# Eight relu evictions per supertile moved from ScalarE to VectorE in a fused attention and FFN kernel

## The reference, cut to what is computed

```python
xn = layernorm(x)
# attention branch: q, k, v = split(xn @ Wqkv); attention over the lags 0, 1, 2, 4, ...;
# a 7-tap causal convolution over v; linear attention with elu(q)+1, elu(k)+1; then @ Wo
x_prev = shift_by_one_token(xn)
xr = mu_r * xn + (1 - mu_r) * x_prev
xk = mu_k * xn + (1 - mu_k) * x_prev
r = sigmoid(xr @ W_r.T)
k = xk @ W_k.T
k_act = square(relu(k))
ffn = r * (k_act @ W_v.T)
y = x + (xn + attention) + ffn
```

## Time and profile before

| what | us |
|---|---|
| median of 2 runs (2105.49 to 2115.18) | 2110.34 |
| the profiled execution's own time | 2121.86 |
| its span on core 1, the slowest, which the rows are from | 2120.3 |
| spans of the eight cores | 2078.9 to 2120.3 |
| mean granted TensorE clock of core 1 | 0.839 |

### The profile page before, as it was taken

One profiled execution on the slowest core, in us unless ns is written; L12 is line 12 of the kernel. 1 busy time (PEld: TensorE's weight loads), 2 busy tenths in 40 slices (PEclk: granted clock), 3 DMA queues, 4 the chain that ended last, 5 costly groups with the idle time before them and its releaser, 6 DMA issues.

```text
span 2120.3 us, 32484 instructions; the slowest of 8 cores (2078.9 to 2120.3 us)
## 1 busy us (share of the span) xinstructions
PE 1433.3 (68%) x10400; PEld 815.1 (38%) x10400; DVE 1232.1 (58%) x1968; ACT 745.1 (35%) x992; POOL 118.4 (6%) x137
## 2 busy tenths in 40 slices
PE   0068778687887787868878715575757575758485
PEld 0024334334333343333343303343545463728282
DVE  0086487684884866848747466372727262636354
ACT  0034142242242422422324215253635362625263
POOL 0001001001010010010100100000000000000000
PEclk9999799788898797888879757788878887979797
DMA  8821320320403204113021262414141414132221
GB/s 150 112 70 50 79 105 16 111 89 15 154 31 90 100 11 129 71 36 133 31 77 73 60 164 56 129 31 130 31 130 30 130 32 129 32 113 48 80 71 40
DMA packets 75229, 168.08 MB, mean 79 GB/s; under 512 B 38080, under 2 KB 38208, under 8 KB 69952
## 3 DMA queue, kind: packets, MB, share of 16 engines
q1 hardware_dynamic: 59632, 100.98, 16.7%
q0 software_dynamic: 15440, 65.02, 11.6%
HBM read 113.55 MB, written 67.11 MB: 85 GB/s over the span
## 4 chain that ended last, share of the span: by engine, by line
PE 43%; DVE 18%; DMA 17%; issue 11%; ACT 9%; DVEq 1%; SPq 1%; POOL 0%; ACTq 0%; POOLq 0%
DVE s_cv L282 6%; PE PS L541 6%; DMA s_vr<-vt_sp 6%; PE PS L598 5%; PE PS L569 5%; PE PS L906 3%; PE PS L1071 3%; PE PS L1074 3%; PE PS L467 3%; DMA s_q<-q_sp 3%; PE PS L955 3%; PE PS L628 2%; PE PS L958 2%; PE PS L910 2%; DMA s_wq<-wqkv 2%
## 5 line engine op out<-in xcount | busy, mean ns | idle before, releaser
L467 PE MATMUL PS<-s_xnfm,s_wq 128*128 128x512 bf16 x1536 | 383.9, 413 | 60.8 <-ACT s_vh L490 43.2
L282 DVE SCALAR_TENSOR_TENSOR s_cv<-s_vh,s_cw,s_cv 128x512 bf16<-128x512 bf16 x384 | 328.1, 854 | 43.7 <-DVE s_cv L282 4.1
L926 DVE RECIPROCAL s_rr<-PS 128x512 f32<-128x512 f32 x64 | 214.9, 3358 | 126.8 <-PE PS L910 126.6
L973 ACT ACTIVATE s_er<-PS,s_con 128x768 bf16<-128x768 f32 (+5 forms) x256 | 226.8, 889 | 163.4 <-PE PS L958 162.9
L467 PEld LDWEIGHTS PS<-s_xnfm,s_wq 128*128 128x128 bf16 x1536 | 157.9, 104 | 283.7 <-issue 131.7
L955 PE MATMUL PS<-s_q,s_kr 128*128 128x128 bf16 x1288 | 186.1, 230 | 96.5 <-DMA s_q<-q_sp 79.4
L958 PE MATMUL PS<-s_id,s_mlog 128*128 128x128 bf16 x1288 | 187.0, 231 | 0.0
L906 PE MATMUL PS<-s_er,s_vr 128*128 128x128 bf16 x1288 | 119.0, 225 | 98.2 <-ACT s_er L973 68.1
L955 PEld LDWEIGHTS PS<-s_q,s_kr 128*128 128x128 bf16 x1288 | 132.9, 104 | 102.9 <-issue 100.6
L393 PE MATMUL PS<-s_id,s_xnb 128*128 128x128 bf16 x256 | 29.9, 283 | 159.9 <-DVE s_st L379 134.2
L958 PEld LDWEIGHTS PS<-s_id,s_mlog 128*128 128x128 bf16 x1288 | 133.5, 104 | 0.1
(11 more groups left out here) (99 smaller groups left out, 1827.7 us busy)
## 6 DMA issues: line engine op xcount, KB each, us to landing
s_xa<-x SPq DMA_DIRECT2D x32, 512.0 KB, 4.3
s_xb<-x SPq DMA_DIRECT2D x32, 512.0 KB, 4.4
p_sp<-s_p POOLq DMA_DIRECT2D x32, 512.0 KB, 3.7
s_p<-p_sp SPq DMA_DIRECT2D x32, 512.0 KB, 13.8
y<-s_p SPq DMA_DIRECT2D x32, 512.0 KB, 3.9
q_sp<-s_qk POOLq DMA_DIRECT2D x8, 1024.0 KB, 4.3
k_sp<-s_qk POOLq DMA_DIRECT2D x8, 1024.0 KB, 4.3
vt_sp<-s_vt POOLq DMA_DIRECT2D x8, 1024.0 KB, 8.1
```

The source lines that it names most:

```text
L282: cinc(e.scalar_tensor_tensor(s1_cv[:, ch, :], src, s_cw[:, ch, j:j + 1], s1_cv[:, ch, :], ALU.mult, ALU.add))
L467: last = e.matmul(bank(bsel, 0, 512), s1_wq[:, kc, 128 * m:128 * (m + 1)], s1_xnfm[:, kc, 1:513], start=(kc == 0), stop=(kc == 7), skip_gr ...
L926: cinc(e.reciprocal(s2_rr[:, 512 * half:512 * half + 512], PS[:, 512 * (6 + half): 512 * (6 + half) + 512]))
L973: return e.activation(s2_er[:, eslot, 0:128 * n], src, AF.Exp, bias=s_con[:, 0:1], scale=s_con[:, 1:2])
```

## The change

The relu of the W_k product moves from ScalarE (activation) to VectorE (tensor_scalar with max 0), with the same operands. The square on POOL, the reuse of the PSUM banks and the first four groups of the W_v product now wait for VectorE's count.

```diff
-            wts.append(("act", ka_evac[m - 4]) if m >= 4 else ("act", rg_evac[4 + m]))
+            wts.append(("dve", mx_done[m - 4]) if m >= 4 else ("act", rg_evac[4 + m]))
             W("tensor", kmm_fn, waits=wts, inc="pe")
             kmm = pl.val["pe"]
-            W("scalar", (lambda m, bsel: lambda e: e.activation(
-                s1_xr[:, m, :], bank(bsel, 0, 512), AF.Relu))(m, bsel),
-                waits=[("pe", kmm)], inc="act")
-            ka_evac[m] = pl.val["act"]
+            W("vector", (lambda m, bsel: lambda e: e.tensor_scalar(
+                s1_xr[:, m, :], bank(bsel, 0, 512), 0.0, None, ALU.max))(m, bsel),
+                waits=[("pe", kmm)], inc="dve")
+            mx_done[m] = pl.val["dve"]
             W("gpsimd", (lambda m: lambda e: e.tensor_tensor(
                 s1_xr[:, m, :], s1_xr[:, m, :], s1_xr[:, m, :], ALU.mult))(m),
-                waits=[("act", ka_evac[m])], inc="pool")
+                waits=[("dve", mx_done[m])], inc="pool")
...
-                wts.append(("act", ka_evac[4 + m]))
+                wts.append(("dve", mx_done[4 + m]))
```

## The result

The changed kernel takes 2148.01 us in the median (11 runs, 2143.6 to 2166.11) where the kernel before took 2107.46 beside it (8 runs, 2101.21 to 2118.95). The ratio is 1.0202, with a 95% interval of 1.0167 to 1.0238: the kernel is slower, and whether by more or by less than 2% is not settled. The forecast was 2154 us. In some executions of these kernels the cores of one die run at a lower granted clock and the time is some per cent longer; all times and ratios here leave those out. The ratios are worked out from the single runs and not from the medians, and the two can differ by 0.2 or 0.3%.

The account below looks back on a forecast made before the run. TensorE was taken as the bound, with a hole of 2.2 us per supertile waiting for the square. Later start plus clock, (3.8 + 1.7) x 8 = 44 us, on the 2110.34 us median gave 2154 us; range 2130 to 2180.

Parts of the forecast that it names:

- What bounds the stage: Second supertile's chain from W_k through relu and square to W_v: TensorE is the bound, with one hole, 2.2 us per supertile.
- The hand-over from VectorE to TensorE: Between W_k and W_v: late relus and four squares in a row start TensorE 3.8 us later in each supertile.
- its cover: Head 3 ends about 361.7, and the bank is needed at 363.8 at the earliest: covered by about 1.4 us.
- Relus 4 to 7. These are what the change costs: Relus queued behind head 2 on VectorE: all four late, in a row from 351.36, delaying squares and W_v by 3.8 us.
- they cost nothing: Relus 0 to 3, behind head 1 on VectorE: run at TensorE's pace with 3 us of cover, at no cost.
- The clock: W_v product behind the longer hole: starting at 1.2 GHz costs 2.1 us per supertile, less 0.4 paid now, adding 1.7.
- Nothing downstream takes the shift back: Stages behind the W_v product, from transposes to stores, start from what ended ahead of them and recover none of the delay.
- the fourth rival: First sweep's later stages: a changed clock pattern gives the loss back, 2119 us with all of it returned; chance 0.05.
- The squares alone: Rival 1, hole ahead of W_v: the deeper hole costs no more clock, 30 us in all, 2141 us; chance 0.22.
- Relu and square in turns: Rival 2, relus 4 to 7 and POOL's squares: they take turns, 64 us in all, 2174 us; chance 0.13.
- Head 3 holding up the squares: Rival 3, last two squares: each waits for a head 3 operation, 1.8 us more, 2168 us; chance 0.09.
- The squares' steady 1.04 us does not show the turn in which POOL waits: POOL's squares beside two-input VectorE operations: minimum 1.03, median 1.04 us, so the rows show only VectorE stretching.

Follow-up runs that it names:

- The filled hole: Changed kernel with 24 matmuls whose results nobody reads in TensorE's hole between the W_k and W_v products: 2134.31 us, ratio 1.0142.
- the two with the product split: W_v's first two groups split, steps 0 to 6 ahead: kernel before, 2085.21 us; all relus on VectorE with head 2 ahead of them, 2099.15 us.

## Why the prediction was right, point by point

**What bounds the stage** was right: the chain through relu, square and W_v, with TensorE's hole of 2.1 us as its only gap. The wait was forecast to grow to about 48 us in 8 waits and is 46.0.

**The hand-over from VectorE to TensorE** was worked out as 3.8 us and measured as 3.58 (all cores). Its pieces: the relu 0.69 and 0.69; head 2 with one square beside it 6.62 and 6.30 (351.97 to 358.27); four squares 4.32 and 4.52; the hand-over 0.25 and 0.25. The stall of a head per square was taken as 0.76 from two heads beside eight squares; one square cost 0.44 here, and three cost 0.69 each in the experiment with relus 4 and 5 on ScalarE. Head 3, forecast at about 8 us, takes 7.20 (360.68 to 367.87), and its cover held.

**"Relus 4 to 7. These are what the change costs"** was wrong as an attribution, although the sum came out. Relus 4 to 7 alone on VectorE give a ratio of 0.9986. What fails is "they cost nothing" of relus 0 to 3: the cover of 3 us was read for the relus themselves and not for head 2, which the fourth of them holds from 335.7 to 344.7. The prediction has this delay in its next paragraph ("only then does head 2 start") and counts it, so the path and the sum are right; it books the whole cost on relus 4 to 7, because the wait appears only behind head 2.

**The clock** was taken as 2.1 us per supertile less 0.4 paid already. Over eight cores it is 16.20 - 13.97 = 2.23 less 0.29, so 1.94 against 1.7. The prediction read the 0.4 from core 1, which had two slow starts in eight. The filled hole shows that this term is the clock's and not a second wait.

**"Nothing downstream takes the shift back"** held as far as the traces can tell. The W_r product and the rest together are 0.55 us shorter per supertile, 4 us of 44, a tenth of what the fourth rival needed, and even these can't be put down to the change, since the rest is as short in two kernels whose W_v product runs near full clock. The rest does react to something, though. In the three kernels without a hole of 2 us ahead of the W_v product (the hole filled, and the two with the product split) the rest takes 91.84 to 92.00 us; in the other six it takes 91.17 to 91.55. The projections alone do not explain it: their matmuls have a mean of 409 ns with the hole filled and 404 with the product split. The cause stays open.

**The total** came out 3 us low: a loss of 41 us by the medians, against the forecast's 44. The other 3 us between 2154 and 2148 are the starting point, 2110.34 us in the two runs that the forecast had and 2107.46 beside the result.

**Rivals 1 to 3.** The squares alone: refuted, the W_v product takes 15.3 to 16.9 us in all 64 cases and not 14. Relu and square in turns: refuted by the line of the relu in the changed kernel (durations in ns: shortest, median, longest), with squares running beside many of them:

```profile
L577 DVE TENSOR_SCALAR s_xr<-PS x64: 679/691/693, 200.1 to 1212.0; 128x512 bf16<-128x512 f32 x64
```

Head 3 holding up the squares: this happens, at a fifth of the rival's 1.8 us. These are one operation of head 3 and the eighth square, in the second supertile of core 0:

```profile
361.39 1.34 DVE L282 SCALAR_TENSOR_TENSOR s_cv<-s_vh,s_cw,s_cv 128x512 bf16<-128x512 bf16 x1
362.15 1.48 POOL L581 TENSOR_TENSOR s_xr<-s_xr 128x512 bf16<-128x512 bf16 x1
```

The operation is stretched from 0.75 to 1.34 us by the seventh square, and the eighth square, which begins while it runs, ends 0.90 us after it and takes 1.48 us instead of 1.04. It takes 1.48 in all 64 cases. The seventh, beside L280, takes 1.09. Four squares in a row so take 4.52 us instead of 4 x 1.04 = 4.16, that is 0.36 more.

**"The squares' steady 1.04 us does not show the turn in which POOL waits"** was a misreading of the earlier trace rows. The least and the median are 1.03 and 1.04, but the longest is 1.43, and the earlier trace rows has a square of 1.21 us that begins at 344.79, while the operation begun at 344.35 is running. Over the eight cores of the kernel before, 124 of 512 squares take more than 1.1 us. Taken one by one they show both turns. Where a square begins 0.1 to 0.52 us after an L282 operation that keeps its 0.75 us (85 cases), the square ends 0.90 us after that operation in every case, however long it had been under way, and takes 1.13 to 1.54 us. Where it begins within 0.1 us of the operation (213 cases), the square takes 1.04 us in the median and the operation 1.62. Both this and the relu's row agree with what the Trainium skill says in "SBUF — State Buffer", section "Who interferes with whom": the port pair that the two engines share is an exclusive lock, and a VectorE operation with at most one SBUF input outside the two-port modes stays clear of it.

**The chances** put 0.52 on a loss of over 2% and 0.46 on one within. At 1.0202, with an interval to both sides, the result is on that line, where the forecast had placed it.

## What to carry to other kernels

Moving work to an engine that has time on average is decided by the order of that engine's list. For each moved instruction ask two things: what is queued ahead of it when its input is ready, and what it holds back while it waits for its input. The second is easily missed, because the instruction itself looks punctual. A wait that TensorE gains is to be priced with the matmuls behind it: here a hole 3.6 us longer cost 5.5. And where a product waits for the last of several inputs, the contraction steps that need only the earlier ones can go ahead; that was worth 1.2% here, with ScalarE keeping its relus.

## What the hardware showed that was not expected

The loss behind a hole is 0, 0.29, 1.69 and 2.23 us for holes of 0.55, 2.1, 4.9 and 5.7 us, as means over 64 products each. The means hide that single products differ: of the holes of 2.1 to 2.3 us in the kernel before, 53 of 64 are free, and the other 11 cost 1.6 to 1.7 us each.

Matmuls whose results nobody reads made the kernel 0.6% faster than the same kernel with the hole left empty. The price is that the projections, some 30 us later, ran more at 1.2 GHz (409 ns mean against 404 over the eight cores).

A VectorE operation with two SBUF inputs and a POOL square take turns, and either can be the one that waits. The convolution operation takes 0.75 us alone and 1.62 in the median when a square begins within 0.1 us of it; the square takes 1.04 us alone and up to 1.54 when it begins later than that beside an operation under way. So the median of the squares (1.04 us in both kernels) says nothing about the last one, which is the one that TensorE waits for: in the changed kernel it takes 1.48 us every time. L280, with one SBUF tile as input, is stretched as well, from 0.34 to 0.62 us beside the seventh square. The relu from PSUM neither suffers (0.68 to 0.69 us) nor disturbs: the 256 squares that have only relus beside them take 1.03 to 1.04 us.
